# Two-step queries in the wide attention, a pipelined own projection, and a ScalarE front for the quantised feed-forward

## The reference, cut to what matters

```python
xn  = layernorm(x)                                   # 32 x 128 per sequence
q   = (xn @ Wq)  * 64**-0.5                          # Wq: 128 x 1024, one 64-wide slice per head
k,v = split(context @ Wkv)                           # Wkv: 256 x 2048; plus one learned null key and value
out = softmax(q k^T) v                               # 257 + 1 keys
x  += layernorm(out @ Wout) * ln_scale + ln_bias
```

## Time and profile before

| | |
|---|---|
| time, median of 3 | 3746.05 us |
| profiled execution: time, span | 3756.79 us, 3755.0 us |
| TensorE busy, weight loads | 3271.3 us (87%), 2755.7 us (73%) |
| VectorE, ScalarE, GpSimd busy | 2625.7 us (70%), 1746.5 us (47%), 1242.9 us (33%) |
| mean granted TensorE clock | 0.93 of 2.4 GHz |
| L2_xattn's loop (first mix to last) | 1890 to 3262 us of the span |
| L1_xattn's own projections | 1045 to 1107 us |
| start | 0 to 57 us |

### The profile page before, as it was taken

How to read it: one execution, slowest core, us unless ns; L and a number is a source line. 1 busy time by engine, 2 the same in 40 slices (tenths; PEclk the granted TensorE clock), 3 DMA queues, 4 the chain that set the end, 5 groups by cost and what they waited for, 6 DMA issues and landing times. The chain is left out here.

```text
span 3755.0 us, 107408 instructions
## 1 busy us (share of the span) xinstructions
PE 3271.3 (87%) x40334; PEld 2755.7 (73%) x40336; DVE 2625.7 (70%) x7574; ACT 1746.5 (47%) x4346; POOL 1242.9 (33%) x1791
## 2 busy tenths in 40 slices
PE   5887999999968888887899999999999999874766
PEld 4675898988946666644789999998989989744344
DVE  6784999999948888756555556565556655469766
ACT  4331777777727777755423233333233333223353
POOL 3562888888813333311400000000000000145032
PEclk8996999999979999988899999999999999968687
DMA  4000000000012222200175656665566666355000
GB/s 126 5 0 37 1 0 0 0 0 0 1 42 75 76 74 75 66 12 6 33 144 120 130 126 128 125 131 123 125 129 127 129 125 130 65 104 82 1 3 25
DMA packets 375343, 253.50 MB, mean 68 GB/s; under 512 B 118660, under 2 KB 371544, under 8 KB 374392
## 3 DMA queue, kind: packets, MB, share of 16 engines
q1 hardware_dynamic: 370680, 244.92, 30.0%
q10 hardware_dynamic: 4352, 4.20, 0.5%
HBM read 233.01 MB, written 15.75 MB: 66 GB/s over the span
## 5 line engine op out<-in xcount | busy, mean ns | idle before, releaser
L2232 ACT ACTIVATE L_xattn_prob<-psum,L_xattn_nmax 128x258 f32<-128x258 f32 x512 | 239.4, 473 | 853.0 <-DVE L_xattn_nmax L2274 853.0
L2366 PE MATMUL psum<-L_xattn_ctxT,L_xattn_q_ctx 128*128 128x257 f32 x2048 | 525.0, 389 | 9.4 <-DMA L_xattn_ctx<-ctx_dram 8.0
L1067 PE MATMUL psum<-L_ffn_share,L_ffn_prob 128*128 128x128 f32 x4096 | 491.0, 279 | 45.9 <-DVE L_ffn_prob L1000 38.4
L1067 PEld LDWEIGHTS psum<-L_ffn_share,L_ffn_prob 128*128 128x128 f32 x4096 | 473.4, 193 | 59.6 <-DVE L_ffn_prob L1000 46.3
L883 POOL TENSOR_TENSOR L_ffn_sums<-L_ffn_sims 128x1024 f32<-128x1024 f32 x256 | 485.3, 1912 | 85.8 <-DVE L_ffn_prob L1000 85.8
L2395 PEld LDWEIGHTS psum<-L_xattn_probT,L_xattn_ctx 32*128 32x128 f32 x16384 | 469.8, 187 | 53.1 <-DVE L_xattn_q_ctx L2265 46.3
L2395 PE MATMUL psum<-L_xattn_probT,L_xattn_ctx 32*128 32x128 f32 x16384 | 494.8, 273 | 7.9 <-issue 2.6
L2208 POOL TENSOR_TENSOR L_xattn_z_var<-L_xattn_z_mv,L_xattn_z_eps 128x1 f32<-128x1 f32 x32 | 6.1, 192 | 1285.2 <-DVE L_xattn_z_mv L2300 1255.9
L2366 PEld LDWEIGHTS psum<-L_xattn_ctxT,L_xattn_q_ctx 128*128 128x128 f32 x2048 | 361.3, 191 | 65.8 <-issue 10.0
L925 ACT ACTIVATE psum<-L_ffn_sums,L_ffn_bias 128x512 f32<-128x512 f32 x512 | 339.5, 687 | 89.6 <-DVE L_ffn_prob L1000 85.8
L1000 DVE SCALAR_TENSOR_TENSOR L_ffn_prob<-L_ffn_sums,L_ffn_best,psum 128x512 f32<-128x512 f32 x512 | 358.8, 744 | 7.0 <-ACT psum L925 3.8
(11 more groups left out here) (454 smaller groups left out, 6250.4 us busy)
## 6 DMA issues: line engine op xcount, KB each, us to landing
L_xattn_ctx<-ctx_dram SPq DMA_DIRECT2D x512, 256.0 KB, 5.4
L_xattn_ctxT<-ctx_T_dram SPq DMA_DIRECT2D x128, 257.0 KB, 3.1
L_xattn_k_all<-ctx_T_dram SPq DMA_DIRECT2D x128, 128.5 KB, 2.1
L_xattn_v_all<-ctx_dram SPq DMA_DIRECT2D x128, 128.0 KB, 2.2
L_attn_qkv_scratch<-L_attn_qkv SPq DMA_DIRECT2D x24, 256.0 KB, 2.8
L_attn_rows<-L_attn_qkv_scratch SPq DMA_DIRECT2D x24, 256.0 KB, 5.3
start_raw<-ctx_dram ACTq DMA_DIRECT2D x16, 256.0 KB, 12.0
L_xattn_v_rows<-L_xattn_v SPq DMA_DIRECT2D x8, 256.0 KB, 2.3
```

Of the source, the lines that this page charges most:

```text
L1067: last = nc.tensor.matmul(pair(2 * s)[:, c * P:(c + 1) * P], prob[:, h % RING, c * P:(c + 1) * P], share[:, h % RING, :], start=(h == 0 an ...
L2232: ins = nc.scalar.activation(prob[:, s, g, :], scores(s)[:, g, :], ACT.Exp, bias=nmax[:, s, g:g + 1], accum_out=total[:, s, g:g + 1])
L2366: last = nc.tensor.matmul(scores(s)[:, g, 0:CTX], q_ctx[:, p, c, b, h:h + 4, :].rearrange("p h n -> p (h n)"), ctxT[:, b, c, :], start=(c ...
```

## The change

Four edits: (1) the start no longer forms or copies `m_h` and does not load Wk^T; (2) `wide_tokens` loads `wq_cross` and `wk_cross` on SyncE, and the loop makes a group of four heads of one tile (a unit u of 128, four for each tile) in two steps: `project` (two products, 128 rows), a scaled copy by ScalarE, `to_context` (eight products over 64 rows, halves in turn, into banks 2 and 3), two copies of 512 columns by VectorE; (3) `own_qkv` is unrolled into 8 groups of 4 tiles, with ScalarE normalising; (4) in the front of L2_ffn ScalarE normalises.

```diff
 start():
-            load(sp, [(wq[:, :, :], dram[f"{name}_WqT"]), (wk[:, :, :], dram[f"{name}_WkT"])], qk_in)
+            load(sp, [(wq[:, :, :], dram[f"{name}_WqT"])], q_in)
-            for k in range(4):
-                copy_m(k)
-            pe.wait_ge(qk_in, 32)
-            for k in range(4):
...
-                        last = nc.tensor.matmul(m_bank(k, e)[:, i * CD:(i + 1) * CD], wq[half(e), 2 * k + i, :],
-                                                wk[half(e), 2 * k + i, :], start=True, stop=True)
 own_qkv(), ScalarE, VectorE, TensorE:
+            normalise(0)
+            for g in range(GROUPS):
+                if g + 1 < GROUPS:
+                    normalise(g + 1)
+                turn_copy(g)
+                if g >= 1:
+                    q_copy(g - 1)
+            q_copy(GROUPS - 1)
...
+            for g in range(GROUPS):
+                front.dve_moments(dve, 0, only=group(g))
+                if g >= 3:
+                    copies(g - 3)
...
+            turn(0)
+            pe.wait_ge(w_in, 48)
+            for g in range(GROUPS):
+                if g + 1 < GROUPS:
+                    turn(g + 1)
+                project(g)
 wide_tokens():
+        @block.sync
+        def _(sp):
+            load(sp, [(wq_cross[:, :, :, :], core.dram[f"{name}_Wq_cross"]),
+                      (wk_cross[:, :, :, :], core.dram[f"{name}_Wk_cross"])], qk_cross_in)
 wide_attention():
+    AHEAD = BT + 1
+    head_bank = lambda u: core.psum[:, 6 + u % 2, 2 * P:4 * P]
+    ctx_bank = lambda a, e, c: core.psum[:, 2 + e, 256 * a + c * P:256 * a + c * P + P]
 ScalarE:
+        def copy_heads(u):
+            act.wait_ge(heads_made, u + 1)
+            nc.scalar.activation(q_heads[:, u % 2, :, :], head_bank(u)..., ACT.Copy, scale=64 ** -0.5).then_inc(heads_out, 1)
                 following = next_seq(t, b, p, after)
+                if t * BT + b + AHEAD + 1 < GROUPS:
+                    copy_heads(t * BT + b + AHEAD + 1)
                 if following:
                     exps(following[0] * BT + following[1], 0)
 VectorE:
+        def q_copy(u):
+            t, j = place(u)
+            dve.wait_ge(q_made, u + 1)
+            for c in range(2):
+                nc.vector.tensor_copy(q_ctx[:, t % 2, c, :, 4 * j:4 * j + 4, :], ...).then_inc(q_out, 1)
+                if t * BT + b + AHEAD < GROUPS:
+                    q_copy(t * BT + b + AHEAD)
                 if following:
                     maxes(*following[0:2], 0)
-                pieces = q_pieces(t, b, p, after)
-                for piece in pieces[0:3]:
-                    q_copy(*piece)
 TensorE:
+        def project(u):
+            t, j = place(u)
+            if u >= 2:
+                pe.wait_ge(heads_out, u - 1)
+            for a in range(2):
+                last = nc.tensor.matmul(head_bank(u)[:, a * P:(a + 1) * P], wq_cross[:, j, a, :], tokens(t), start=True, stop=True)
+            last.then_inc(heads_made, 1)
+        def to_context(u):
+            t, j = place(u)
+            pe.wait_ge(heads_out, u + 1)
+            if u >= 1:
+                pe.wait_ge(q_out, 2 * u)
+            for a in range(2):
+                for c in range(2):
+                    for e in range(2):
+                        half = slice(64 * e, 64 * e + 64)
+                        last = nc.tensor.matmul(ctx_bank(a, e, c), wk_cross[half, j, a, c * P:(c + 1) * P],
+                                                q_heads[half, u % 2, a, :], start=True, stop=True)
+            last.then_inc(q_made, 1)
 TensorE, score(), s = 1:
+            elif 0 in groups:
+                pe.wait_ge(q_out, 2 * min(t * BT + b + AHEAD, GROUPS))
 TensorE, tile(), iteration n:
+                if n + AHEAD < GROUPS:
+                    pe.wait_ge(exped, 2 * n + 2)
+                    to_context(n + AHEAD)
                 if following:
                     score(*following, 0, True)
+                if b or before:
+                    pe.wait_ge(mix_out, n)
+                if n + AHEAD + 1 < GROUPS:
+                    project(n + AHEAD + 1)
                 ahead = before and b == 0
                 if ahead:
                     values(t - 1)
...
-                if pieces:
-                    pe.wait_ge(q_out, t * PIECES + 4 * b + PIECES + 8)
+                if n + AHEAD + 1 < GROUPS:
+                    pe.wait_ge(heads_out, n + AHEAD + 2)
                 mix(t, b)
 before the loop, TensorE:
-        for k in range(PIECES):
-            q_piece(0, k)
-        for k in range(4):
-            q_piece(1, k)
+        pe.wait_ge(qk_cross_in, 32)
+        project(0)
+        for u in range(AHEAD):
+            project(u + 1)
+            to_context(u)
 quantised_ffn(), VectorE:
             front.dve_moments(dve, 0, only=chunks[0])
+            weight_peaks()
             front.dve_moments(dve, 0, only=chunks[1])
-            front.dve_normalise(dve, 0, only=chunks[0])
-            weight_peaks()
             split_bias()
             front.dve_moments(dve, 0, only=chunks[2])
             greatest(1, 3, 1)
-            front.dve_normalise(dve, 0, only=chunks[1])
+            front.dve_moments(dve, 0, only=chunks[3])
             nc.vector.tensor_copy(ones_b[:, :], core.ones[0:3, :])
             steps_of(1, 3, 1)
-            round_weights()
-            front.dve_moments(dve, 0, only=chunks[3])
             peak_of(0)
             peak_of(1)
-            front.dve_normalise(dve, 0, only=chunks[2])
-            front.dve_normalise(dve, 0, only=chunks[3])
+            round_weights()
             peak_of(2)
             peak_of(3)
```

More of the change, by code:

```diff
@@ new lines, in project @@
+            def project(g):
+                pe.wait_ge(xnT_done, g + 1)
+                four = xnT[:, g % 2, :, :].rearrange("p s w -> p (s w)")
+                if g >= 2:
+                    pe.wait_ge(q_done, g - 1)
+                nc.tensor.matmul(q_bank(g), w[:, 0:D], four, start=True, stop=True).then_inc(q_made, 1)
+                if g >= 2:
+                    pe.wait_ge(k_done, g - 1)
+                nc.tensor.matmul(k_bank(g), w[:, D:2 * D], four, start=True, stop=True).then_inc(k_made, 1)
+                if g >= 2:
+                    pe.wait_ge(v_done, g - 1)
+                for s in range(PACK):
+                    last = nc.tensor.matmul(v_bank(g)[:, s * P:(s + 1) * P], xnT[:, g % 2, s, :], w[:, 2 * D:3 * D],
+                                            start=True, stop=True)
+                last.then_inc(v_made, 1)
@@ L2139, in next_seq, with place @@
         return (t, b + 1, p) if b + 1 < BT else (t + 1, 0, 1 - p) if after else None
[L2141 to L2145 removed]
+    def place(u):
+        return u // G, u % G
     @block.sync
@@ L2411, in tile @@
                     pe.wait_ge(v_copied, 4 * t)
-                elif b:
-                    pe.wait_ge(mix_out, t * BT + b)
-                for piece in pieces[0:3]:
-                    q_piece(*piece[0:2])
-                if ahead:
                     output(t - 1)
@@ L2419, in tile @@
                     score(*following, 1, True, range(0, 1))
-                for piece in pieces[3:4]:
-                    q_piece(*piece[0:2])
                 if following:
                     score(*following, 1, True, range(1, 2))
-                if pieces:
-                    pe.wait_ge(q_out, t * PIECES + 4 * b + PIECES + 8)
-                if before and b == 0:
+                if n + AHEAD + 1 < GROUPS:
+                    pe.wait_ge(heads_out, n + AHEAD + 2)
+                if ahead:
                     pe.wait_ge(z_copied, t)
```

193 lines of the change are left out of this document (98 added, 95 removed).

## The result

| | before | after |
| --- | --- | --- |
| median of four runs | 3745.97 us | 3716.14 us |
| lowest to highest | 3743.5 to 3755.57 | 3711.28 to 3720.33 |
| profiled execution | 3756.79 (span 3755.0) | 3720.33 (span 3717.9) |

The ratio is 0.9915, 95% interval 0.9893 to 0.9937: 24 to 40 us. The forecast of 3673 (3650 to 3708) is missed on the slow side.

What follows compares the result with a forecast made beforehand. The prediction took the L2_xattn loop to be bound by TensorE's own work. Gains of 43 + 24 + 5 + 1 = 73 us took the profiled 3756.8 to 3683.8; less 10.7 for the median, 3673 us, range 3650 to 3708.

Steps and rivals of the forecast that it cites:

- what bounds the kernel now: Opening step: TensorE is busy 87% of the span, and L2_xattn's loop is bound by TensorE's own work.
- the ring: Loop's dependency chain through copies, maxima, exponentials and to_context: 8.7 us plus up to 0.2, hidden behind TensorE's 8.91.
- The loop's term: L2_xattn's loop with its head: a gain of 43 us, between 15 and 55.
- rival (c): Loop's to_context: the row halves take turns, costing 1.78 + 0.10 us; total 3778 us; chance 3%.
- The switch: Loop, TensorE: changing the number of rows in use costs 0.10 us; the change adds one per iteration.
- Tile-first iterations: Loop: 30 iterations of 15.25 us, each saving 0.49, with about 0.13 lost again.
- The first tile and what stands ahead of it: Ahead of the loop: preparation hardly matters behind a 5.47 us transfer wait; only the iteration behind it gains, about 1 us.
- The forecast's 46 for the iterations: Loop: TensorE's saving summed over iterations, 93 x 0.34 + 30 x 0.49 = 46 us.
- Own projections: Own projections stage: TensorE bounds at 3.57 us a group; 62.3 us becomes 38, a gain of 24.
- rival (b): Own projections: the clock stays low there, costing 24 us; total 3697 us; chance 9%.
- Start: Kernel start: without the product copies U's copies start at once; gain 5 us, between 4.1 and 8.
- Quantised front: Front of L2_ffn: peak of x ready earlier, but TensorE still waits for bias rows; gain 1 us, between 0 and 5.

Runs made afterwards that it cites:

- experiment 5: Kernel before, with each iteration's five context loads spread out instead of issued together: 3747.15 us, ratio 0.9992; loop 1399.7 against 1404.4.
- experiment 3: Changed kernel, each replica load bringing one of its eight row blocks after the first tile: 3671.37 us, ratio 0.979 to the kernel before.
- 4: Changed kernel, same context bytes, but the five loads of an iteration spread instead of issued together at the mix's end: 3673.65 us, ratio 0.9799.
- 8: Changed kernel, context loads still in one burst but released by to_context's end, 1.0 to 1.1 us later: 3691.67 us, ratio 0.9843.
- 6: Kernel before, its context loads held for a later score, issued 2.0 us later: 3757.65 us, ratio 1.0017.
- 9: Changed kernel, loads in one burst, query copies shared between VectorE and ScalarE: 3699.91 us, ratio 0.9881.
- 11: Changed kernel with context loads spread and query copies shared between VectorE and ScalarE: 3674.11 us, ratio 0.9797.
- 7: Kernel before, TensorE waiting at each wide-loop iteration's head for VectorE's reciprocal of the same sequence: 3750.08 us, ratio 0.9997.
- experiment 10: Kernel before, one wait for VectorE's copy of the first query piece added before the third quarter of the scores: 3777.1 us, ratio 1.0089.

## Why the prediction was wrong

**The step that failed** is in "what bounds the kernel now": nothing stands between TensorE's groups, so the loop is bound by TensorE's own work, and a saving in it is a saving in time. What may be late next was then looked for among engines (the ring, VectorE, ScalarE); the supply of instructions has no term in the sum and no rival. The loop's term was a gain of 43 us, and the loop came out 3 us longer. The trace of before had the sign of it, four stops of 0.65 to 1.03 us inside mixes, which were passed over. With the loads spread, and not one instruction of TensorE's other, the same kernel runs at 3673.65, within a microsecond of the forecast (3671 if its ratio is taken to the first runs of the kernel before); the late packets cost 42 us (3716.14 - 3673.65). That the two agree so closely is luck in part, since some terms were too large and others too small:

**The loop, TensorE.** to_context over 64 rows: 16 records in 1.16 with the last one's tail of 0.27, that is 0.89, as taken (0.90). The halves of the rows run beside each other; rival (c) falls. The switch was undercounted. to_context lasts 1.09 to the next start, 0.20 above its records, and each half of the scores 0.09 to 0.10 above eight records at 0.218, together 0.39; before, it was 0.20 an iteration. The group of 64 rows put between thus costs 0.19 beyond its records, not 0.10: query work 1.53 instead of 1.45, an iteration 9.00 instead of 8.91, about 11 us over 123. The Trainium skill, TensorEngine Tiling (Array Packing), Key Properties, says that a change of the tiling mode drains the engine; the trace agrees that it costs, about 0.1 us on each side of the inserted group.

**Tile-first iterations**: 14.84, where the sum had 14.9 (15.25 - 0.49 + 0.13); 30 x 0.41 = 12 us. The 90 other iterations behind the first tile give 21 (9.24 to 9.00). The first tile and what stands ahead of it give 4, where 1 was forecast: the wait of 5.4 for a context transfer is gone, but the way to the first mix is 1.7 longer, and a stop of 2.8 stands in the first iteration. That is the 37 of experiment 5, and with 5 for the stops of the kernel before the 41.7 by which the spread loop is shorter than the old one; forecast 43. The forecast's 46 for the iterations, less 4 for the ring, measured 33. The ring's slack was enough: no wait for exponentials in front of to_context.

**Own projections**: forecast 62.3 to 38; by the same points (VectorE's first moments at 1040.17 to the end of its last copy at 1074.68) 34.5. The term that was mis-sized is the four transposes, 0.44 (1055.36 to 1055.80) instead of 0.9, since each is one record and not two: a group is 3.05, not 3.57. The granted clock was 0.95 over the 30 us ahead of the next stage, where it had been 0.73; rival (b) falls.

**Start**: 3.9 of 5. **Quantised front**: 2.8 in the profile; over the seven traces with the new front it takes 136.0 on average, over the six with the old one 137.7, so nearer 1.7, with the wait for the bias rows as described. **L1's context attention** came 4.3 us shorter, which no step had. In the traces with the new own projections it takes 480.3 to 483.1, with the old ones 484.1 to 484.8. The granted clock explains the spread within the first group (0.993 of full speed over the stage at 480.3, 0.986 at 483.1), not the gap: with the old ones it is 0.989 to 0.992. The gap grows evenly over the stage, by 0.03 us for each of the 128 sequences; why is open.

**Shown and not shown.** Shown: the loop's loss is packets of instructions that come late because of the context loads. Every stop stands at a packet's first instruction, and all 23 go when the loads are smaller (experiment 3) or spread (4); how many come depends on when the loads are issued (8, and weakly 6) and on when the query copies end (9). Shown in part: in the new code more packets are asked for late (16 of 29 at 7.4 us or later, against 7 of 28 in the old code), the copies set their time (11), and in the old code too packets asked for at 8.4 or later are late (5 of 7). Open: why in the new code packets that are asked for as early as in the old one (4.6 and 4.8 in the table's middle column) are late as well, and why packets get in among the loads in the old code and hardly ever in the new one. Stops could not be made at will in the old code (6, 7, 10).

## What to carry to other kernels

A loop without gaps between its groups may still lose what it saves: look for rows of one group broken by "issue" and for the instruction queue's packets near them, above all where a few microseconds of loads are issued in one go and a dense run of small matmuls (here 256 instructions in 3.8 us) follows. The cure cost nothing here (ratio 0.9992 on the kernel before): give each load of the burst its own event to wait for, if its buffer has iterations in hand. And when an experiment gives the expected time, read its trace before believing the reason (experiment 10).

## What the hardware showed that was not expected

- TensorE's instructions come in packets of 16 KB (229 packets, 3.75 MB), one for each 256 of its records here with its waits counted, each 0.9 to 1.9 us long, and TensorE went on 2.5 to 2.9 us after a late one's start. With 1.31 MB of loads ahead of them, packets for the last 80 instructions of a mix started 11.0 us after the preceding mix's start, where undisturbed it was 4.8 and 7.8 (the table's last two columns), and TensorE stopped 1.0 to 2.0 us. The Trainium skill, DMA: Bandwidth & Descriptors, Queues, rings and completion order, says that each DMA engine takes turns between the queue rows that have work, one packet at a time; by that an instruction packet would be held up by one packet of a load and not by the whole row of them. The trace of the new code doesn't agree (25 of 29 packets start at 10.6 to 11.5, as the loads drain at 11.2), that of the old one rather does (23 of 28 start at 4.2 to 8.6); the measurement decides, and what makes the difference is part of what is open.
- A group of 64-row products between groups of 32 and of 128 rows costs 0.19 us beyond its records.
- Four transposes of 128x128 follow each other at 0.11 us (0.44 for the four), the price of a record.
